# A later turn-back, another bank order and a later first normalisation in a gated layer

## The reference, cut to what matters

```python
def reference(x, ctx, g_xattn, g_ffn, ssm_kernel, D, ln_w, ln_b, W1, b1, W2, b2):
    x = x + tanh(g_xattn[0]) * mixer(ctx, ctx, layernorm(x), ssm_kernel, D, 8)
    x = x + tanh(g_ffn[0]) * ffn(layernorm(x), ln_w, ln_b, W1, b1, W2, b2)

def mixer(k, v, q, taps, D, head_dim):            # 64 heads of 8 channels
    kv = einsum('bhil,bhjl->bijhl', k, v)         # products of channels
    y = causal_long_convolution(kv, taps)         # by FFT, 1024 positions
    out = y + kv * D
    return einsum('bijhl,bhil->bjhl', out, q)     # laid out as (b, channels, 1024)

def ffn(x, ...):                                  # every step is rounded to bf16
    h = layernorm(x) * ln_w + ln_b
    h = mx_quant(h) @ mx_quant(W1).T + b1         # 1024 -> 4096
    h = gelu(h)
    h = mx_quant(h) @ mx_quant(W2).T + b2         # 4096 -> 1024
    return x + h

def mx_quant(x):   # blocks of 32 values share a power of two: the scale from the block's peak,
                   # then round to integers, clip to 8 bits, multiply by the scale again
```

## Time and profile before

| | before |
|---|---|
| median of three runs | 1961.39 us (1959.43 to 1961.52) |
| profiled execution, own time | 1956.56 us |
| its span, first to last instruction | 1954.8 us |
| mean granted TensorE clock | 0.992 of full speed |
| busy share of PE, DVE, ACT, POOL | 96%, 86%, 48%, 46% |

### The profile page before, as it was taken

One profiled execution on the slowest core, in us unless ns is written; L12 is line 12 of the kernel. 1 busy time (PEld: TensorE's weight loads), 2 busy tenths in 40 slices (PEclk: granted clock), 3 DMA queues, 4 the chain that ended last, 5 costly groups with the idle time before them and its releaser, 6 DMA issues. The chain is left out here.

```text
span 1954.8 us, 28607 instructions
## 1 busy us (share of the span) xinstructions
PE 1868.0 (96%) x11432; PEld 1466.9 (75%) x11432; DVE 1679.1 (86%) x1928; ACT 940.4 (48%) x1227; POOL 891.8 (46%) x645
## 2 busy tenths in 40 slices
PE   6999999999998999999995997999999999999998
PEld 5988888888987889888884565666677766666773
DVE  6889999989897989999978898989888888889843
ACT  5555556555645555545523443444445534434440
POOL 3888889787887989999960000000000000000000
PEclk9999999999999999999999998999999999999999
DMA  7665657777665767766657421222122211221112
GB/s 244 216 207 170 191 168 229 234 246 263 217 209 154 250 191 236 247 198 218 189 209 286 154 70 55 66 76 76 44 76 76 76 66 54 66 76 53 45 44 76
DMA packets 165477, 294.24 MB, mean 151 GB/s; under 512 B 106144, under 2 KB 106144, under 8 KB 157152
## 3 DMA queue, kind: packets, MB, share of 16 engines
q1 hardware_dynamic: 165344, 292.41, 45.8%
HBM read 222.05 MB, written 45.68 MB: 137 GB/s over the span
## 5 line engine op out<-in xcount | busy, mean ns | idle before, releaser
L373 PE MATMUL y_ps<-kk_hi,slab 128*128 128x352 f32 (+6 forms) x3328 | 890.8, 351 | 31.9 <-DMA slab<-taps_scratch 18.3
L373 PEld LDWEIGHTS y_ps<-kk_hi,slab 128*128 128x128 f32 x3328 | 594.1, 189 | 102.6 <-issue 31.6
L373 PE MATMUL y_ps<-kk_lo,slab 128*128 128x512 f32 (+6 forms) x1664 | 580.6, 349 | 0.0
L1079 PE MATMUL l_ps<-f_xq_T,w_rest 128*128 128x256 bf16 x3136 | 348.4, 273 | 7.7 <-DMA f_xq_T<-f_hq 6.3
L1079 PEld LDWEIGHTS l_ps<-f_xq_T,w_rest 128*128 128x128 bf16 x3136 | 307.1, 98 | 47.6 <-issue 6.8
L373 PEld LDWEIGHTS y_ps<-kk_lo,slab 128*128 128x128 f32 x1664 | 314.1, 189 | 34.5
L860 POOL TENSOR_TENSOR terms<-terms 128x768 f32<-128x768 f32 x127 | 325.0, 2559 | 9.9
L1142 ACT ACTIVATE arena<-l_ps,b_c 128x256 bf16<-128x256 f32 x496 | 206.7, 472 | 248.0 <-PE l_ps L1079 242.8
L1380 POOL TENSOR_TENSOR f_rstd<-f_var_eps,f_neg_half 128x1 f32<-128x1 f32 x28 | 15.3, 547 | 672.8 <-DVE f_var_eps L1200 672.8
L479 ACT CAST kk_hi<-raw_room 128x2304 fp32r<-128x2304 f32 x64 | 135.9, 2123 | 195.7 <-DVE raw_room L617 127.9
L1097 PE MATMUL acc_ps<-w_T,arena 128*128 128x512 bf16 x1024 | 226.2, 379 | 0.0
(11 more groups left out here) (147 smaller groups left out, 2201.6 us busy)
## 6 DMA issues: line engine op xcount, KB each, us to landing
slab<-taps_scratch SPq DMA_DIRECT2D x128, 512.0 KB, 4.8
arena<-in_w_m SPq DMA_DIRECT2D x32, 1024.0 KB, 6.6
arena<-x_scratch SPq DMA_DIRECT2D x60, 512.0 KB, 3.6
raw_room<-in_ctx_e SPq DMA_DIRECT2D x64, 384.0 KB, 3.3
arena<-in_w SPq DMA_DIRECT2D x22, 1024.0 KB, 6.6
x_tile<-in_x_t SPq DMA_DIRECT2D x32, 512.0 KB, 4.9
out_t<-arena SPq DMA_DIRECT2D x32, 512.0 KB, 2.6
w_scratch<-arena SPq DMA_DIRECT2D x22, 512.0 KB, 7.2
```

The lines of the kernel that those rows point to most:

```text
L373: mm = nc.tensor.matmul(y_ps[:, y_base + begin:y_base + end], slab[s][:, half, d * P:(d + 1) * P], kk_part[s][:, begin - d * PAIR:end - d ...
L1079: mm = nc.tensor.matmul(l1_ps[bank % L1_BANKS][:, a, :], w1_tile(b)[:, k, a * P:(a + 1) * P], inputs[:, k, :], start=(k == 0), stop=(k == ...
```

## The change

It has four parts.

1. `turn_back(t-1)` moves on PE from behind stretch 0 to behind stretch 1 of the odd head. DVE's `residual(t-1)` moves from ahead of `times_q(h, 0)` and `low_half(h+1)` to behind both.
2. `first_banks` gets another order: the banks of group 1 that need no late tile come forward, and the others are mixed in two to one.
3. DVE quantises the first late weight tile as soon as it is clipped, and the first two peaks come two and one tiles later.
4. On ACT, `first_norm` of the tiles 8 and 9 moves from the end of group 2 into group 3, behind bank 6.

```diff
-LAG = 6
@@ PE
-                    if h % TILE_HEADS == 1 and i == 0 and t >= 1:
+                    if h % TILE_HEADS == 1 and i == 1 and t >= 1:
                         turn_back(t - 1)
@@ DVE, mixer
                     make_kk(h + 1)
-                if h % TILE_HEADS == 1 and t >= 1:
-                    residual(t - 1)
                 times_q(h, 0)
                 if h + 1 < heads:
                     low_half(h + 1)
+                if h % TILE_HEADS == 1 and t >= 1:
+                    residual(t - 1)
@@
-    first_banks = []
-    for b in range(FILL, banks + LAG):
-        first_banks += [(0, b)] if b < banks else []
-        first_banks += [(1, b - LAG)] if b >= FILL + LAG else []
+    first_banks = [(g, b) for g in range(2) for b in range(FILL, KEPT)]
+    for b in range(KEPT, banks):
+        first_banks += [(0, b)]
+        first_banks += [(1, (b + KEPT) // 2)] if (b - KEPT) % 2 == 0 else []
+    first_banks += [(1, b) for b in range(banks) if b >= FILL and (1, b) not in first_banks]
@@ ACT
                         if g == 2 and b == 11:
                             for s in range(GROUP):
                                 first_norm(GROUP * (g + 1) + s)
+                        if g == 3 and b == 6:
+                            for s in range(GROUP):
+                                first_norm(GROUP * (g + 1) + s)
@@
                 for s in range(GROUP):
-                    if g != 1 and g + 2 < groups:
+                    if g not in (1, 2) and g + 2 < groups:
                         first_norm(GROUP * (g + 2) + s)
@@ DVE, FFN
                 weight_ints(j)
-                if j > KEPT:
+                if j > KEPT + 1:
                     weight_quant(j - 1)
                 weight_scales(j)
                 weight_clip(j)
-                if j in (KEPT, 11):
-                    peak(0, 0 if j == KEPT else 1)
+                if j == KEPT:
+                    weight_quant(j)
+                if j in (8, 12):
+                    peak(0, j // 4 - 2)
```

## The result

The changed kernel takes 1970.01 us (median of four runs, 1969.48 to 1971.84) where the kernel before took 1960.54 in the same comparison: 1.005 times as long, 95% interval 1.0038 to 1.0062. That is 9.5 us slower, clear of the 0.2%. The direction and nearly all the signs in the trace were as forecast; the forecast size was 20.9, more than double. Its profiled span is 1968.7 us, 13.9 more than the profiled span before.

The account below looks back on a forecast made before the run. PE, busy 96% of the span, was taken as the bound, in turn with DVE in long stretches of heads. The terms 7 - 7.5 - 10 - 6 + 2.65 - 7.0 gave -20.9, added to the median 1961.39: 1982 us, range 1962 to 1989.

Parts of the forecast that it names:

- turn-back waits, heads 37 to 44: PE's waits ahead of the turn-backs go; 7 us gained, bounds 0 and 12.1, the latter from PE's busy time.
- heads 9 to 23: Eight odd heads pay for the residual behind `low_half`, slack takes a part: 7.5 us lost.
- heads 35 and 45 to 59: Nine odd heads pay for the residual behind `low_half`, with little slack: 10 us lost.
- last job's load: Job 21's load, queued behind tile 29's store, lands late, so DVE waits 5.3 us: 6 us lost with head 61's residual.
- FFN's start: DVE quantises the first late tile without waiting 3.01 us for a gelu; group 2 comes earlier: 2.65 us won.
- later `first_norm`: Groups 3 and 4: DVE's statistics run late, so bank 7 of group 4 comes later: 7.0 us lost, bounds 0 and 8.
- DVE takes over before that: Heads 37 to 44: DVE becomes the bound before PE's 12.1 us are won; with POOL the stretch takes 129.7 us.
- POOL, behind by then, adds up to one more instruction: Heads 37 to 44: POOL adds up to 1.58 us in some two heads, 3 us.
- residual's 1.13 us: `low_half` ends no earlier for starting earlier, so the residual behind it costs 1.13 us per odd head where DVE counts.
- (a): Odd heads: the end of `low_half` doesn't hang on POOL, so each loses only 0.51 us; 1969.6 us, chance 0.16.
- (b): Odd heads: DVE takes the residual for nothing as `low_half` ends earlier; faster, 1953 us, chance 0.16.
- (c): Whole kernel: costs and gains cancel, no effect worth a name; 1957.5 to 1965.3 us, chance 0.08.

Follow-up runs that it names:

- banks_only: Only parts 2 and 3 (bank order, first quantisation at once, later peaks) put into the kernel before: 1958.67 us, 0.9987.
- residual_mid: Kernel before with the turn-back late as in part 1, but the residual between `times_q(h, 0)` and `low_half(h+1)`: 1946.82 us, 0.9924.
- the three parts alone: Kernel before with only part 1: 1966.17 us; only parts 2 and 3: 1958.67 us; only part 4: 1968.25 us.

## Why the prediction was wrong in its size

Most of the mechanisms were right, one term was mis-sized, and another less so. Forecast against measured, in us:

| term | forecast | measured in the profiles |
|---|---|---|
| turn-back waits, heads 37 to 44 | +7 | +11.1, and +4.7 more in executions near the median |
| heads 9 to 23 | -7.5 | -8.6 |
| heads 35 and 45 to 59 | -10 | -6.8 (head 36: 1.1, heads 45 to 61: 5.7) |
| last job's load | -6 | -5.3 |
| FFN's start | +2.65 | +2.95; alone, timed, +2.45 |
| later `first_norm` | -7.0 | -6.4 from group 2's start to bank 7 of group 4; alone, timed, -7.1 |

The profiles' terms, with 0.9 us by which this execution's head 0 began later, make up the 13.9 between the spans.

- **The turn-back waits: "7 us gained, with 0 and 12.1 as bounds"** is the step that failed, and it failed twice. "DVE takes over before that" didn't come true: the stretch took 125.56 us instead of the 129.7 that I had added up for DVE, PE is busy in 122.44 of it, and DVE's busy time is only 0.7 above before. So 11.1 us were won in the profile. And the bound of 12.1 came from one profile in which the clock held behind three of the four waits; I then added the sum to a median 4.8 us above that execution without asking what the 4.8 were. Two profiles with the same mixer show 4.7 in these heads, with the lower clock behind the waits of the heads 39 and 43, and a third shows 2.9. With 15.8 instead of 7 the sum is -12.1. A wait that is taken away also takes away its chance of a slow restart, and that part isn't in a quick profile. That the median executions of the kernel before have this lower clock is inferred from a profiled one of banks_only near its median, from the two groups of times and from the runs' mean clocks; no profile of such an execution was taken.
- **"POOL, behind by then, adds up to one more instruction"** went the other way. In the iterations 39, 43, 53 and 57 `low_half` came ahead of POOL's L861 instead of behind it. DVE's and then POOL's order of time in head 53 of the changed kernel:

```profile
856.82 2.63 DVE L622 TENSOR_TENSOR kk_lo<-raw_room,kk_hi 128x2304 fp32r<-128x2304 f32 x1 [0.51 <-ACT kk_hi L478]
```

```profile
857.12 3.77 POOL L861 TENSOR_TENSOR terms<-terms 128x640 f32<-128x640 f32 x1
```

DVE starts 0.30 us ahead and is done in 2.63 us; POOL's instruction takes 3.77 instead of 1.57. The Trainium skill, "SBUF — State Buffer", section "SBUF: two separate sides", says that whichever of the two starts first blocks the other. I had used it for one order only; here the trace agrees with it for the other. The heads behind them pay next to nothing: head 40 and head 54 are as long as before, head 44 is 0.3 longer and head 58 1.1 shorter. That is most of why the ten us forecast for heads 35 and 45 to 59 came out as 6.8: with 1.13 in each of nine heads I had left no room for a change of order. The rest isn't even: head 46 loses nothing, since its `low_half` ends 1.60 us ahead of its start, and the heads 47 and 48 together lose 2.6.
- **The residual's 1.13 us** was right where the order stayed: residual_mid shows that the place ahead of `low_half` is free and the one behind it is not, with some 20 us between them.
- **The last job's load, the FFN's start and the later `first_norm`** came out as worked out, each within 0.7 us.
- Of the rivals, (a) and (b) fall with the 2.41 us behind POOL that held in the other odd heads in which DVE is the bound; (c) with the three parts alone, each of which has an effect clear of noise. That (a)'s 1969.6 us lies beside the measured 1970.01 is chance: its condition, an end of `low_half` that doesn't hang on POOL, is not what the trace shows.

## What to carry to other kernels

Where two engines block each other, an instruction's place is judged by what its neighbours wait for: the same 1.2 us was free ahead of the blocked instruction and cost 1.1 behind it, head after head. Before a sum from one profile is added to a median, the gap between the two has to be explained; if it lies in stretches behind PE's waits, removing those waits is worth more than the profile says. And an engine that works in order should not stand at an instruction whose input comes through a DMA while ready work is queued behind it: moving `norm_again` by four banks won 3 us, moving only the normalisation that PE did not wait for lost 7.

## What the runs showed of the hardware that I had not expected

PE's granted clock behind waits of the same length was not the same in each execution: after 3.7 us it was at 1.00 over the head's window in two executions of the same mixer, at 0.92 in a third and at 0.84 in two more, and the eight transposes behind it took 1.07 us in the first three and 1.94 in the others. And a few tenths of a microsecond decide which of DVE's and POOL's instructions blocks the other: `low_half` took 2.63 us where it started 0.30 ahead of POOL's L861, which then took 3.77 instead of 1.57; where it started 0.13 behind it (head 55) it took 3.86.
